# Fused cross-attention and quantised FFN: the ten probability transposes in one block, both output halves ahead of the second scores

## The reference, cut to what matters

```python
def _L0_xattn_ref(x, context, context_mask, Wq, Wk, Wv, Wo):   # x normalised, 2x2048x512; context 2x77x384
    q = (x @ Wq).reshape(B, N, 16, 32).transpose(0, 2, 1, 3)
    k, v = context @ Wk, context @ Wv                          # reshaped in the same way
    scores = jnp.einsum('bhid,bhjd->bhij', q, k) * scale       # 16 heads, 77 keys each
    attn = jax.nn.softmax(jnp.where(mask, scores, max_neg), axis=-1)
    out = jnp.einsum('bhij,bhjd->bhid', attn, v).transpose(0, 2, 1, 3).reshape(B, N, 512)
    return out @ Wo
x = x + jnp.tanh(g_xattn[0]) * _L0_xattn_ref(_layernorm(x), ctx_768, mask_BxS2_bf1, ...)
x = x + jnp.tanh(g_ffn[0]) * _L0_ffn_ref(_layernorm(x), ...)   # gate, up, down with fake-quantised weights
return x                                                        # and activations
```

## Time and profile before

| | us |
|---|---|
| median of 3 runs | 638.42 (637.68 to 639.74) |
| the profiled execution | 636.91 |
| its span | 635.10 |
| TensorE busy | 613.6 (97%) |
| VectorE busy | 510.3 (80%) |
| ScalarE busy | 352.1 (55%) |
| GpSimd busy | 197.1 (31%) |

### The profile page before, as it was taken

How to read it: one execution, slowest core, us unless ns; L and a number is a source line. 1 busy time by engine, 2 the same in 40 slices (tenths; PEclk the granted TensorE clock), 3 DMA queues, 4 the chain that set the end, 5 groups by cost and what they waited for, 6 DMA issues and landing times. The chain is left out here.

```text
span 635.1 us, 12602 instructions
## 1 busy us (share of the span) xinstructions
PE 613.6 (97%) x3841; PEld 461.9 (73%) x3862; DVE 510.3 (80%) x954; ACT 352.1 (55%) x512; POOL 197.1 (31%) x416
## 2 busy tenths in 40 slices
PE   8999999999999999999999986999999999899997
PEld 6699999999999999999999864444444444444544
DVE  6688788888988888899988657788888888866764
ACT  4264567566566656656664343555555554365553
POOL 7112333333333333323421202111111110057775
PEclk9999999999999999999999998999999999999999
DMA  8748422222222223312411000286446110099623
GB/s 305 207 115 249 121 59 68 58 66 47 58 60 58 66 58 68 78 36 77 97 42 50 25 0 1 48 239 221 132 137 211 26 29 12 0 341 418 266 109 123
DMA packets 85206, 69.61 MB, mean 110 GB/s; under 512 B 64915, under 2 KB 67373, under 8 KB 85165
## 3 DMA queue, kind: packets, MB, share of 16 engines
q1 hardware_dynamic: 79377, 52.13, 29.6%
q10 hardware_dynamic: 5788, 16.98, 7.4%
HBM read 32.48 MB, written 21.36 MB: 85 GB/s over the span
## 5 line engine op out<-in xcount | busy, mean ns | idle before, releaser
L1343 ACT ACTIVATE sb_silu<-ps_g,sb_sgu 128x512 f32<-128x512 f32 x88 | 60.5, 687 | 72.1 <-PE ps_g L1430 42.8
L1430 PE MATMUL ps_g<-sb_xqT,sb_wgu 128*128 128x512 bf16 x344 | 89.3, 379 | 1.0 <-DVE sb_xqT L1386 0.6
L1430 PE MATMUL ps_u<-sb_xqT,sb_wgu 128*128 128x512 bf16 x346 | 89.4, 379 | 0.3
L603 ACT COPY sb_pT<-ps_p 128x512 f32<-128x512 f32 (+1 forms) x96 | 46.4, 521 | 69.6 <-PE ps_p L1042 69.6
L1053 PE MATMUL ps_o<-sb_vblk,sb_pT 128*128 (+4 forms) x640 | 79.1, 270 | 3.3 <-ACT sb_pT L603 2.5
L1401 DVE SCALAR_TENSOR_TENSOR sb_h<-ps_u,sb_sgu,sb_silu 128x512 f32<-128x512 f32 (+1 forms) x88 | 66.1, 751 | 19.8 <-PE ps_u L1430 19.4
L1053 PEld LDWEIGHTS ps_o<-sb_vblk,sb_pT 128*128 128x128 f32 (+1 forms) x640 | 76.9, 191 | 4.7 <-ACT sb_pT L603 3.5
L986 PE MATMUL ps_q<-sb_xT_hi,sb_wq_hi 128*128 128x256 f32 x256 | 77.9, 304 | 0.0
L988 PE MATMUL ps_q<-sb_xT_hi,sb_wq_lo 128*128 128x256 f32 x256 | 72.3, 282 | 0.0
L987 PE MATMUL ps_q<-sb_xT_lo,sb_wq_hi 128*128 128x256 f32 x256 | 72.2, 282 | 0.0
L1636 PE MATMUL ps_z<-sb_wdT,sb_hq 128*128 128x512 bf16 x324 | 71.4, 379 | 0.3
(11 more groups left out here) (227 smaller groups left out, 1331.0 us busy)
## 6 DMA issues: line engine op xcount, KB each, us to landing
h_spill<-sb_h SPq DMA_DIRECT2D x4, 2816.0 KB, 8.8
sb_h<-h_spill ACTq DMA_DIRECT2D x16, 704.0 KB, 7.1
out_dram<-sb_wgu SPq DMA_DIRECT2D x31, 256.0 KB, 2.0
sb_x<-in_x_dram ACTq DMA_DIRECT2D x1, 4096.0 KB, 18.3
sb_w_in<-in_L_ffn_w_gate_dram SPq DMA_DIRECT2D x11, 256.0 KB, 2.6
sb_w_in<-in_L_ffn_w_up_dram SPq DMA_DIRECT2D x11, 256.0 KB, 2.6
sb_x<-in_x_dram SPq DMA_DIRECT2D x2, 1024.0 KB, 14.9
sb_x<-in_x_dram SPq DMA_DIRECT2D x2, 512.0 KB, 5.0
```

The source lines that it names most:

```text
L1343: act.activation(silu[(j * KI + i) % 2][:, :, :].rearrange("p t n -> p (t n)"), p_g[(j * KI + i) % 2][:, :], ACT.Silu, scale=sgu[:, i:i + ...
L1430: last = pe.matmul(banks[(j * KI + i) % 2][:, :], wgu[:, what, k, i * P:(i + 1) * P], xqT[j][:, k, :], start=(k == 0), stop=(k == KD - 1))
```

## The change

`p_o` becomes two views, one in each of the banks `p_p[0]` and `p_p[1]`; the bank that held the outputs now takes chunk 2 of the transposes (`p_c2`). TensorE issues all ten transposes after one another and both halves of the outputs after one another, ahead of scores 1; transposes of chunks 0 and 1 wait for the normalisations of the tile before, outputs 1 no longer waits for a normalisation. In slot 1 the first part of the queries comes ahead of the transposes. ScalarE copies all three chunks and then takes the absolute value. VectorE does reciprocal and normalisation of outputs 1 ahead of the maximum of scores 1, which now stands next to its subtraction, and `x_part` ahead of `stats_end`. The numbers of operations stay, but for one memset more at the start.

```diff
...
 p_ob = pb("o", [P, 512])
-p_o = p_ob[:, 0:HH * VW].rearrange("p (h d) -> p h d", h=HH)
+p_c2 = p_ob[:, 0:2 * P].rearrange("p (k n) -> p k n", k=2)
+p_o = [a[:, :, :].rearrange("p k n -> p (k n)")[:, 0:HH * VW].rearrange("p (h d) -> p h d", h=HH)
+       for a in p_p]
+p_pT = [p_p[0], p_p[1], p_c2]
 p_y = pb("y", [P, D])
...
             act.wait_ge(l_v[0], 16 * SLOT0[KB])
-        for c, (k0, k1) in enumerate(CHUNKS):
-            if c == 2 and runs(n - 4, NT - 1):
-                wait(act, g_nb2, n - 3)
-                wait(act, v_xmax, n - 3)
-                if isinstance(n, int) and n >= PLANES_FREE:
-                    act.wait_ge(v_xlo, NT)
-                else:
-                    wait(act, v_x1, n - 2)
-                act.activation(xabs(n - 4), row(n - 4), ACT.Abs, bias=nb2[:, span(n - 4)],
-                               scale=rs2[:, span(n - 4)]).then_inc(a_abs, 1)
-            if runs(n - 1, NT):
+        if runs(n - 1, NT):
+            for c, (k0, k1) in enumerate(CHUNKS):
                 wait(act, t_p, 3 * (n - 1) + c + 1)
                 wait(act, t_o, 2 * (n - 1) - (c == 0))
-                act.copy(pT[:, k0:k1, :], p_p[c % 2][:, 0:k1 - k0, :]).then_inc(a_p, 1)
+                act.copy(pT[:, k0:k1, :], p_pT[c][:, 0:k1 - k0, :]).then_inc(a_p, 1)
+        if runs(n - 4, NT - 1):
+            wait(act, g_nb2, n - 3)
+            wait(act, v_xmax, n - 3)
+            if isinstance(n, int) and n >= PLANES_FREE:
+                act.wait_ge(v_xlo, NT)
+            else:
+                wait(act, v_x1, n - 2)
+            act.activation(xabs(n - 4), row(n - 4), ACT.Abs, bias=nb2[:, span(n - 4)],
+                           scale=rs2[:, span(n - 4)]).then_inc(a_abs, 1)
         for half in range(2):
...
         wait(dve, v_o, 2 * n + half)
-        dve.reciprocal(rden[:, half, :], p_o[:, :, HD]).then_inc(v_rec, 1)
+        dve.reciprocal(rden[:, half, :], p_o[half][:, :, HD]).then_inc(v_rec, 1)
...
         dve.tensor_tensor(o_sb[:, half * HH * HD:(half + 1) * HH * HD]
-                          .rearrange("p (h d) -> p h d", h=HH), p_o[:, :, 0:HD],
+                          .rearrange("p (h d) -> p h d", h=HH), p_o[half][:, :, 0:HD],
                           rden[:, half, :].unsqueeze(2).broadcast_to([P, HH, HD]), ALU.mult)\
...
             outputs_norm(n - 1, 0)
-        if runs(n, NT):
-            scores_max(n, 1)
         if runs(n, NW):
...
         down_part(n, 1)
+        if runs(n - 1, NT):
+            outputs_rec(n - 1, 1)
         if runs(n - 4, NT):
...
             dve.tensor_reduce(xmax[:, span(n - 4)], xabs(n - 4), X, ALU.max).then_inc(v_xmax, 1)
+        if runs(n - 1, NT):
+            outputs_norm(n - 1, 1)
         if runs(n, NT):
+            scores_max(n, 1)
             scores_sub(n, t, 1)
...
             dve.memset(p_p[1][:, 0, :], 0.0).then_inc(v_zero, 1)
+            dve.memset(p_c2[:, 1, :], 0.0).then_inc(v_zero, 1)
             dve.tensor_scalar(sg_1[:, :], sg_e[:, :], 1.0, None, ALU.add).then_inc(v_sig, 1)
...
                 dve.wait_ge(l_x[5], 16)
-        if runs(n - 1, NT):
-            outputs_rec(n - 1, 1)
         if runs(n + 6, NT):
...
             wait(dve, g_nb, n + 5)
-        if runs(n - 1, NT):
-            outputs_norm(n - 1, 1)
-        if runs(n + 6, NT):
-            stats_end(n + 6, t)
         if runs(n + 4, NT):
             x_part(n + 4, t)
+        if runs(n + 6, NT):
+            stats_end(n + 6, t)
...
         wait(pe, a_exp, 2 * n + (1 if c == 0 else 2))
-        wait(pe, a_p, 3 * n + (0, -1, 1)[c])
+        if c < 2:
+            wait(pe, v_o, 2 * n - 1 + c)
+        else:
+            wait(pe, a_p, 3 * n)
         if isinstance(n, int) and n == 0:
-            pe.wait_ge(v_zero, 1)
+            pe.wait_ge(v_zero, 2)
         k0, k1 = CHUNKS[c]
...
             half, j = divmod(k, KB)
-            last = pe.transpose(p_p[c % 2][0:ROWS[j], k - k0, :],
+            last = pe.transpose(p_pT[c][0:ROWS[j], k - k0, :],
                                 prob[t % 2][:, half, P * j:P * j + ROWS[j]], identf[:, :])
...
         wait(pe, a_p, 3 * n + 2 + half)
-        wait(pe, v_o, 2 * n + half)
         b = n // (S // P)
...
             last = pe.matmul(
-                p_o[:, first:end + 1, :].rearrange("p h d -> p (h d)"),
+                p_o[half][:, first:end + 1, :].rearrange("p h d -> p (h d)"),
                 pT[rows, half * KB + j, :],
...
             scores(n, t, 0)
+        opening = isinstance(n, int) and n == 1
+        if opening:
+            queries(n + 2, (t + 2) % 4, 0)
         if runs(n - 2, NT - 1):
...
         if runs(n - 1, NT):
-            prob_transpose(n - 1, (t - 1) % 4, 0)
-            prob_transpose(n - 1, (t - 1) % 4, 1)
-        if runs(n + 2, NT):
+            for c in range(3):
+                prob_transpose(n - 1, (t - 1) % 4, c)
+        if runs(n + 2, NT) and not opening:
             queries(n + 2, (t + 2) % 4, 0)
...
             outputs(n - 1, 0)
+            outputs(n - 1, 1)
         if runs(n, NT):
...
             values_part(1)
-        if runs(n - 1, NT):
-            prob_transpose(n - 1, (t - 1) % 4, 2)
         if runs(n + 2, NT):
             queries(n + 2, (t + 2) % 4, 1)
-        if runs(n - 1, NT):
-            outputs(n - 1, 1)
         if not joined(n + 4):
```

More of the change, by code:

```diff
@@ L906, in slot @@
                             wait(dve, g_nb, n + 5)
-                        if runs(n - 1, NT):
-                            outputs_norm(n - 1, 1)
+                        if runs(n + 4, NT):
+                            x_part(n + 4, t)
                         if runs(n + 6, NT):
                             stats_end(n + 6, t)
-                        if runs(n + 4, NT):
-                            x_part(n + 4, t)
                     dve.sem_inc(v_xmax, 1)
```

## The result

| | before | changed |
|---|---|---|
| median, us | 637.73 (17 runs, 636.47 to 641.02) | 640.09 (17 runs, 638.01 to 644.37) |
| ratio, 95% interval | | 1.0034 (1.0021 to 1.0047) |
| profiled execution, us | 636.91 | 639.10 |
| its span, mean granted clock | 635.1, 0.997 | 637.3, 0.994 |

The account below looks back on a forecast made before the run. The prediction took TensorE to set the pace in the full slots, busy 20.00 of 20 us. Full slots 0, start +1.7 and end -1.95 summed to -0.3 us, 638.1 against the median 638.42, range 636.2 to 641.8.

Parts of the forecast that it names:

- Full slots, 0: Slots 4 to 29: TensorE sets the pace and keeps its instructions, so 0 us; upper bound 2.3 us.
- The circle: Full slots: dependency loop through VectorE and ScalarE, from one first maximum to the next, summed to 11.15 us against 11.12.
- Rival (a): Full slots: the loop through VectorE and ScalarE is longer than the slot; at 11.32 costs 3.95, 642.1 us; chance 0.2.
- The start, +1.7: Slots 1 to 3: outputs wait for copies and slot 2's out_transpose comes late, +1.7 us; bounds +0.5 and +2.5.
- Slot 30 and the chain in slot 31: Slot 30 saves 0.96 us; through scores 1 and the exponential, chunk 1 transposes come at 373.1 instead of 373.36.
- The end, -1.95: Slots 30 to 32: waits before outputs half 1 and chunk 2 go, -1.95 us; bounds -1 and -2.5.
- The sum: Whole kernel: 0 + 1.7 - 1.95 = -0.3 us, giving 638.1 against the median of 638.42.
- (d): Slots 30 to 32: the end gives nothing because late scores 1 and the exponential bound it; +1.7, 640.1 us; chance 0.05.
- (b): Full slots: changes between fp32 and fp32r matmuls cost TensorE time, two of four vanish; 4.5 us, 633.6; chance 0.08.
- (c): Slots 1 to 3: the start costs nothing since queries cover the copies; -1.95 alone, 636.5 us; chance 0.08.
- The extreme of (a): Full slots: GpSimd's 1.04 us split holds up a VectorE instruction each slot; about 24 us, 662; chance 0.02.

Follow-up runs that it names:

- e6: The change with reciprocals and normalisation of outputs half 1 moved behind the second subtraction on VectorE in slots 4 to 29; 638.14 us, 1.0015 to before.
- e10: The change without its slot 1 exception, so queries there stand behind the transposes as in other slots; 637.92 us, 1.0006 to before.
- e1: The change with ten unused matmuls filling TensorE's 2.35 us wait in the last slot; 638.30 us, 0.9997 to before.
- e3: The change with slots 0 and 1 put back to the order of before; 636.63 us, 0.9977 to before.
- e8: e2 with ten unused matmuls filling the last slot's wait of 2.35 us; 635.84 us, 0.9971 to before.
- e9: The change's banks alone, with the order of before in every slot; 636.36 us, 0.9986 to before.
- e0: The changed kernel run again with no edit; 639.16 us, 1.0013 to before.
- e2: The change's banks everywhere, its new order only in slots 30 and 31; 638.48 us, 1.0003 to before.
- e4: e3 with the second scores ahead of both outputs in slot 31; 635.37 us, 0.9964 to before.
- e7: The change with the second scores ahead of both outputs in slot 1; 639.60 us, 1.0022 to before.

## Why the prediction was wrong

- **Full slots, 0.** Right in kind, short by 0.4 us of 289. The circle was summed to 11.15 and measured 11.18, against a slot of 11.10 and not 11.12. It had its slack of some 0.8 us eaten by slot 16, earlier than forecast, and e6 showed by its removal that it was this circle. The step from the first maximum to the second subtraction took 6.85 us (192.85 to 199.70) for the 6.98 of the sum; the term that was too small is the one from the exponential to x_part, 2.82 (200.53 to 203.35) for 2.66, with nothing on record that says why. Rival (a) was the name for it.
- **The start, +1.7.** Right: +1.8, slot 2 at 46.19 less the 0.54 of the late load, 45.65 for 45.6. Its cause was less clearly seen: the prediction took the wait for the copies from slot 30, but didn't set beside it that the exception makes it (e10).
- **Slot 30 and the chain in slot 31.** Right: -0.95; the chunk 1 transposes came 0.22 before their place of before, once both are counted from slot 30 (17.39 for 17.61 us after its start), where 0.26 was forecast.
- **The end, -1.95: the step that failed.** At full clock it is right to a hundredth: slot 31 +0.73 and the last piece -1.74 (6.70 in e1, e3, e6, e8, e9, e10) with -0.95 make -1.96. What the step left out is what it had itself laid out: with scores 1 behind both outputs, TensorE has nothing to do for 2.35 us in the last slot (the prediction's own times say so: scores to 370.3, four transposes of 0.5 us together, and the next ones at 373.1). It priced that as a wait on the chain and went on at full speed; in four profiled executions of seven the granted clock fell behind it and gave 1.5 to 1.6 us of the gain back (slot 31 and the last piece together take 16.89 to 16.96 us, without the fall 15.39).
- **The sum.** At full clock the terms are +1.8, +0.4 and -1.96, +0.2 us, no measurable difference; with the fall +1.8. The first comparison's 1.0034 means 1.3 to 3.0 us, the second's 1.0013 from -0.6 to +2.2. How often the clock fell in the unprofiled runs can be read from their mean granted clock, since each fall of 3.4 us at half lowers it by 0.0027 (1.7 of 636): it is 0.997, 0.994 or 0.995, 0.991 or 0.992, 0.989 with one to four falls, as in the profiled executions. The changed kernel's first 17 runs, at 0.9918, have 0.8 of a fall more than before's 99 (0.9938); at 1.4 us each (before's runs have medians of 636.7 at 0.997 and 641.0 at 0.989) that is 1.1 us. Its 12 runs in e0 (0.9938) have none more. With the 0.5 us between the terms (+0.2) and the forecast (-0.3), some 1.6 of the 2.5 us are accounted for. The rest is open: at an equal mean clock the changed kernel is still 1.3 to 1.4 us slower (639.0 in 7 runs against 637.8 in 47 at 0.994 and 0.995, 640.1 in 13 against 638.7 in 26 at 0.991 and 0.992), and the terms give only 0.2 of that. The landing of the keys, which differs by 2.2 us between profiled executions, could lie behind it; no run separates it.
- **Rivals.** (d) came nearest in time, 640.1, but not by its mechanism: the exponential bounded what followed no more than forecast. (a) was at work, at 0.4 us. For (b) nothing spoke: full slots didn't get shorter. (c) fell: slot 2 was late by 1.8 us. The extreme of (a), the lock between VectorE and GpSimd, showed nowhere: no full slot was above 11.34 us.

## What to carry to other kernels

Price an idle stretch of TensorE twice: as a wait on the chain, and as a risk to the work behind it, since the clock may be granted at half for it; fill it or break it up (moving one group of scores ahead of two groups of outputs made one wait of 2.35 us into three of at most 1.11). Take a change that bundles banks and orders apart: here the banks alone gave the 1.7 us in the last piece, the new order paid only in slots 30 and 31, and a special case written for slot 1 was most of the start's cost. A loop through two engines that is 0.7% longer than the slot stays hidden for ten slots, so look at how an instruction's place in the slot drifts, not at one slot.

## What the runs showed of the hardware

Behind the same 2.35 us of an idle TensorE, in kernels that are alike from slot 30 to the end, the full clock was kept in some executions and lost in others. The changed kernel itself lost it in both of its profiled executions, but three of its 29 runs have a mean clock of 0.997, which leaves room for the fall at the entry of the feed-forward part alone. The fall began when the engine was at work again (0.76 in 376 to 378 us, work from 375.84 on) or at the end of the wait: taken as one stretch, e2's starts at 373.2 (0.80 in 372 to 374), 0.2 us ahead of the first load. Each fall was of one size: what the three windows lack of 1.00, doubled for a level of half and times 2 us, makes 3.4 us (0.24, 0.50 and 0.12 in the first, 0.43 twice in e0, 0.20, 0.50 and 0.16 in e2), and slot 31 and the last piece took 1.5 to 1.6 us longer for it. The clock also fell at the entry of the feed-forward part in all profiled executions, between 388 and 398 us, around the end of 4.25 us without a weight load; by the same sum that is 3.4 us before the change and in most of the others, 6.8 us in e2 and e3. In e4 and e7 a second fall of 3.4 us followed, in the windows from 396 and from 398 us on.

A third place is the same in every kernel here, the way into the down product, where TensorE is idle for 2.30 us. In e1:

```profile
553.14 0.13 PEld L1641 LDWEIGHTS ps_z<-sb_wdT 128*128 128x128 bf16 x2 [2.30 <-issue]
```

```profile
554.00:556.00 2.00, 2.00 (x10) 1.63 (x10) 1.90 (x8) 0.27 (x1) 0.00 (x0) 0.59 0.00 0
556.00:558.00 2.00, 2.00 (x9) 0.99 (x8) 2.00 (x4) 1.96 (x4) 0.00 (x0) 0.56 0.21 45
```

The clock fell behind these 2.30 us in e1, e4, e7 and e8, by 3.4 us each, and stayed at 1.00 in the other nine profiled executions, before the change among them. Together with the seven executions above, a wait of 2.3 us was followed by a fall in 8 of 20 cases. Why in some executions and not in others is open; one such fall more or less is as large as what the change does to the time.
